# Two rows of the batch to a partition in a six-layer cross network

## The reference

```python
def step(x, wb):
    wi, bi = wb
    xw = jnp.matmul(x, wi)
    x_new = x0 * xw + bi + x
    return (x_new, None)
x, _ = jax.lax.scan(step, inputs, (w, b))
```

## Time and profile before

| | |
|---|---|
| median of 3 runs | 1281.35 us (1281.14 to 1282.9) |
| profiled execution | 1280.2 us |
| its span, first to last instruction | 1278.4 us |
| mean granted TensorE clock | 0.782 of full |
| VectorE busy | 1150.2 us, 90% |
| TensorE busy | 780.7 us, 61% |
| ScalarE busy | 102.7 us, 8% |
| moved by DMA | 537.28 MB, 420 GB/s on the mean |

### The profile page before, as it was taken

How to read it: one execution, slowest core, us unless ns; L and a number is a source line. 1 busy time by engine, 2 the same in 40 slices (tenths; PEclk the granted TensorE clock), 3 DMA queues, 4 the chain that set the end, 5 groups by cost and what they waited for, 6 DMA issues and landing times.

```text
span 1278.4 us, 20057 instructions
## 1 busy us (share of the span) xinstructions
PE 780.7 (61%) x9114; PEld 728.6 (57%) x9114; DVE 1150.2 (90%) x526; ACT 102.7 (8%) x345; POOL 4.3 (0%) x17
## 2 busy tenths in 40 slices
PE   8666666555656655556555665665655665665653
PEld 4666566555556655555545565565655654665653
DVE  5999999898988988989889898898998988989896
ACT  3000000000000000000000000000000000000010
POOL 1000000000000000000000000000000000000000
PEclk9877787887877778778787777777777778678677
DMA  9999999999999999999999999999999999999996
GB/s 385 416 380 428 430 431 431 429 427 429 433 429 431 431 430 432 430 431 424 421 424 425 418 427 421 424 425 422 427 424 421 424 423 425 425 423 425 426 421 286
DMA packets 37385, 537.28 MB, mean 420 GB/s; under 512 B 4168, under 2 KB 4168, under 8 KB 4728
## 3 DMA queue, kind: packets, MB, share of 16 engines
q1 hardware_dynamic: 18432, 268.44, 50.1%
q10 hardware_dynamic: 18936, 268.64, 49.3%
HBM read 268.63 MB, written 268.44 MB: 420 GB/s over the span
## 4 chain that ended last, share of the span: by engine, by line
DMA 72%; DVE 15%; PE 8%; issue 3%; ACT 1%; DVEq 0%
DMA out_dram<-tiles 56%; DMA tiles<-in_r_inputs_dram 15%; DVE tiles L286 8%; DVE blocks L264 7%; PE dots L401 6%; ACT spread L197 1%; PE dots L359 1%; PE scratch L339 1%; DMA tiles<-in_L_rec_w_dram 0%; PE strips L334 0%; PE strips L349 0%; ACT c_last L189 0%; PE turned L370 0%; DVE scale L275 0%; DVEq L42 0%
## 5 line engine op out<-in xcount | busy, mean ns | idle before, releaser
L401 PE MATMUL dots<-blocks,weights 128*64 128x128 f32 x7808 | 662.6, 349 | 380.8 <-DVE blocks L264 380.6
L401 PEld LDWEIGHTS dots<-blocks,weights 128*64 128x64 f32 x7808 | 628.7, 185 | 405.3 <-DVE blocks L264 405.2
L264 DVE STREAM_TRANSPOSE blocks<-tiles 128x2048 f32<-128x2048 f32 x256 | 576.0, 2288 | 100.1 <-issue 100.1
L286 DVE SCALAR_TENSOR_TENSOR tiles<-tiles,scale,c_last 128x4096 f32<-128x4096 f32 (+1 forms) x131 | 571.9, 4368 | 0.2
L197 ACT ACTIVATE spread<-dots,group_mask 128x128 f32<-128x128 f32 (+1 forms) x268 | 75.2, 363 | 1062.6 <-PE dots L401 1020.3
L370 PE MATMUL turned<-layer_sel,spread 128*128 128x8 f32 x512 | 68.1, 258 | 85.5 <-ACT spread L197 85.5
L370 PEld LDWEIGHTS turned<-layer_sel,spread 128*128 128x128 f32 x512 | 62.3, 191 | 101.4 <-issue 95.6
L359 PE MATMUL dots<-blocks,weights 128*64 128x64 f32 x768 | 32.4, 266 | 11.0 <-DVE blocks L264 11.0
L359 PEld LDWEIGHTS dots<-blocks,weights 128*64 128x64 f32 x768 | 31.7, 180 | 12.9 <-issue 12.9
L205 ACT ACTIVATE growth<-turned,ones 128x16 f32<-128x16 f32 (+1 forms) x67 | 18.3, 273 | 85.0 <-PE turned L370 85.0
L275 DVE TENSOR_TENSOR_SCAN scale<-growth,cw 128x6 f32<-128x6 f32 x128 | 13.3, 142 | 8.9 <-ACT growth L205 8.9
(11 more groups left out here) (25 smaller groups left out, 11.3 us busy)
## 6 DMA issues: line engine op xcount, KB each, us to landing
tiles<-in_r_inputs_dram SPq DMA_DIRECT2D x128, 2048.0 KB, 14.9
out_dram<-tiles ACTq DMA_DIRECT2D x127, 2048.0 KB, 25.5
out_dram<-tiles ACTq DMA_DIRECT2D x4, 512.0 KB, 7.0
tiles<-in_L_rec_w_dram ACTq DMA_DIRECT2D x1, 96.0 KB
tiles<-in_L_rec_b_dram ACTq DMA_DIRECT2D x1, 96.0 KB
```

The source lines that it names most:

```text
L264: nc.vector.transpose(blocks[:, p % PLACES, :], source).then_inc(blocks_ready, 1)
L286: nc.vector.scalar_tensor_tensor(out=tiles[:, s, at], in0=tiles[:, s, at], scalar=scale[:, u % 2, t, L - 1:L], in1=c_last[:, at], op0=ALU. ...
L401: last = nc.tensor.matmul(dots[at:at + KM * Q, :, :, :], weights[:, c * CH // Q + k:c * CH // Q + k + KM, :], place[:, :, k * Q:(k + KM) * Q],
```

## The change

The rows are laid out in pairs: partition p of a pair of tiles holds rows 2p and 2p + 1 of a stretch of 256 rows, which lie side by side in HBM. There are five slots, each for a pair of tiles (4 MB), so 20 MB in place of 16. A pair is loaded by one DMA of 4 MB, 32 KB to a partition; singles are still loaded one tile at a time. A store is still one tile, now every second row of 16 KB. A slot's next load waits for both of its stores.

Room for this comes from three places. `blocks` has two places in place of four. `c_last` is gone: its lower half is in SBUF (`c_low`), its upper half stays in PSUM (`c_high`, the same memory as `scratch`), and `finish` works in two halves, one with each. `quarter_sum` is gone: the biases are also loaded as rows (`b_rows`, four small DMAs), and TensorE sums six rows with `ones`.

VectorE's order changes. A pair now has all four transposes together, then the finish of tile 1 of the unit before, then the scan and the finish of tile 0 of the same pair. ScalarE spreads, makes the growth, then stores tile 1 of the unit before and tile 0 of this one.

```diff
-PLACES = 4
+PLACES = 2
+PIECES_OF_PAIR = 4
-N_SLOTS = 8
+N_SLOTS = 5
...
+    x_pairs = x.rearrange("(q p t) d -> q p t d", p=P, t=TB)
+    out_pairs = out.rearrange("(q p t) d -> q p t d", p=P, t=TB)
...
+            for q in range(n_all_pairs):
+                s = q % N_SLOTS
...
+                if q >= N_SLOTS:
+                    for t in range(TB):
+                        sp.wait_ge(y_stored[s][t], 16 * stores(q - N_SLOTS))
+                if in_singles(q):
+                    for t in range(TB):
+                        sp.dma_start(tiles[:, s, t, :], x_pairs[q, :, t, :]).then_inc(x_landed[s][t], 16)
+                else:
+                    sp.dma_start(tiles[:, s, :, :], x_pairs[q]).then_inc(x_landed[s][0], 16)
...
             act.dma_start(strips_w, w_strips).then_inc(w_landed, 16)
-            act.dma_start(strips_b, b_strips).then_inc(b_landed, 16)
...
             for j in range(G):
-                nc.scalar.activation(quarter_sum[:, j, :], ones[:], ACT.Copy,
-                                     scale=of_quarter[:, j:j + 1]).then_inc(quarter_sum_ready, 1)
+                act.dma_start(b_rows[j * Q:j * Q + L, :, :], b_halves[j]).then_inc(b_landed[j], 16)
+            act.dma_start(strips_b, b_strips).then_inc(strips_b_landed, 16)
...
+            act.wait_ge(bias_summed, 1)
+            nc.scalar.copy(c_low[:], c_high).then_inc(c_low_ready, 1)
...
-            keep_bias(0)
-            spread_dots(0)
-            keep_bias(1)
             act.wait_ge(cw_all_ready, 1)
             nc.scalar.copy(cw[:], strips[:, 0, 0:LP]).then_inc(cw_ready, 1)
+            spread_dots(0)
             make_growth(0)
             for u in range(1, n_units):
...
+                spread_dots(u)
+                make_growth(u)
+                store(tiles_of(u)[0] - 1)
+                if tiles_of(u)[1] == TB:
+                    store(tiles_of(u)[0])
...
-                parts = 1 if n < n_tiles - 1 else PIECES
+                parts = 2 if n < n_tiles - 1 else STORE_PARTS
...
+                    c = c_low[:, at] if i < parts // 2 else c_high[:, i * width - HALF:(i + 1) * width - HALF]
...
                 wait_tiles(u)
-                transpose_pieces(u, range(2))
+                transpose_pieces(u, range(2 * n_of))
                 if u == 1:
-                    dve.wait_ge(scratch_copied, 2)
+                    dve.wait_ge(c_low_ready, 1)
+                    dve.wait_ge(bias_summed, 2)
                     dve.wait_ge(cw_ready, 1)
-                scan(u - 1)
-                finish(u - 1, 0)
+                if n_before == 1:
+                    scan(u - 1)
+                finish(u - 1, n_before - 1)
                 if n_of == TB:
-                    transpose_pieces(u, range(2, 2 * TB))
-                for t in range(1, n_before):
-                    finish(u - 1, t)
+                    scan(u)
+                    finish(u, 0)
...
-                    last = nc.tensor.matmul(scratch[:, j, :], quarter_sum[0:STRIPS, j, :],
-                                            strips_b[:, h * BANK:(h + 1) * BANK], start=True, stop=True)
+                    last = nc.tensor.matmul(scratch[:, j, :], ones[j * Q:j * Q + L, :], b_rows[j * Q:j * Q + L, h, :],
+                                            start=True, stop=True, tile_position=(j * Q, 0))
...
-                for c in range(PLACES):
-                    pe.wait_ge(blocks_ready, n * PLACES + c + 1)
-                    place = blocks[:, c, :].rearrange("p (t n) -> p t n", t=TB)
+                for c in range(PIECES_OF_PAIR):
+                    pe.wait_ge(blocks_ready, n * PIECES_OF_PAIR + c + 1)
+                    place = blocks[:, c % PLACES, :].rearrange("p (t n) -> p t n", t=TB)
```

More of the change, by code:

```diff
@@ L120, in tiles_of, with in_singles, loads, stores @@
             return u + n_pairs * (TB - 1), 1
+        def in_singles(q):
+            return q * TB < HEAD or q * TB >= n_tiles - TAIL
         def pieces_before(u):
             return 2 * tiles_of(u)[0]
+        def loads(q, t):
+            return sum(1 for k in range(q % N_SLOTS, q + 1, N_SLOTS) if t == 0 or in_singles(k))
+        def stores(q):
+            return q // N_SLOTS + 1
         def weights_of(g):
@@ new lines, in _ @@
+                make_growth(u)
+                store(tiles_of(u)[0] - 1)
+                if tiles_of(u)[1] == TB:
+                    store(tiles_of(u)[0])
+            last_slot = (n_all_pairs - 1) % N_SLOTS
+            for i in range(STORE_PARTS):
+                at = slice(i * D // STORE_PARTS, (i + 1) * D // STORE_PARTS)
+                act.wait_ge(tiles_done, n_tiles + i)
+                act.dma_start(out_pairs[n_all_pairs - 1, :, TB - 1, at],
+                              tiles[:, last_slot, TB - 1, at]).then_inc(y_stored[last_slot][TB - 1], 16)
@@ L241, in _ @@
+            for q in range(n_all_pairs - N_SLOTS, n_all_pairs):
+                s = q % N_SLOTS
+                for t in range(TB):
+                    parts = STORE_PARTS if q * TB + t == n_tiles - 1 else 1
+                    act.wait_ge(y_stored[s][t], 16 * (stores(q) - 1 + parts))
         @block.vector
@@ L261, in transpose_pieces @@
                         dve.wait_ge(blocks_used, p - PLACES + 1)
-                    source = tiles[:, s, c * PIECE:(c + 1) * PIECE] if n_of == 1 else \
-                        tiles[:, s:s + TB, c * CH:(c + 1) * CH]
+                    source = tiles[:, s, first % TB, c * PIECE:(c + 1) * PIECE] if n_of == 1 else \
+                        tiles[:, s, :, c * CH:(c + 1) * CH]
                     nc.vector.transpose(blocks[:, p % PLACES, :], source).then_inc(blocks_ready, 1)
             def wait_tiles(u):
-                first, n_of = tiles_of(u)
-                for n in range(first, first + n_of):
-                    dve.wait_ge(x_landed[n % N_SLOTS], (n // N_SLOTS + 1) * 16)
+                first = tiles_of(u)[0]
+                q, t = first // TB, first % TB
+                dve.wait_ge(x_landed[q % N_SLOTS][t], 16 * loads(q, t))
             def scan(u):
-                first, n_of = tiles_of(u)
+                n_of = tiles_of(u)[1]
                 dve.wait_ge(growth_ready, u + 1)
@@ L279, in finish @@
                 n = tiles_of(u)[0] + t
-                s = n % N_SLOTS
+                tile = tiles[:, n // TB % N_SLOTS, n % TB, :]
                 dve.wait_ge(scale_ready, n + 1)
-                parts = 1 if n < n_tiles - 1 else PIECES
+                parts = 2 if n < n_tiles - 1 else STORE_PARTS
                 width = D // parts
@@ L285, in finish @@
                     at = slice(i * width, (i + 1) * width)
-                    nc.vector.scalar_tensor_tensor(out=tiles[:, s, at], in0=tiles[:, s, at],
-                                                   scalar=scale[:, u % 2, t, L - 1:L], in1=c_last[:, at],
-                                                   op0=ALU.mult, op1=ALU.add).then_inc(tiles_done, 1)
+                    c = c_low[:, at] if i < parts // 2 else c_high[:, i * width - HALF:(i + 1) * width - HALF]
+                    done = nc.vector.scalar_tensor_tensor(out=tile[:, at], in0=tile[:, at],
+                                                          scalar=scale[:, u % 2, t, L - 1:L], in1=c,
+                                                          op0=ALU.mult, op1=ALU.add)
+                    if parts == STORE_PARTS or i == parts - 1:
+                        done.then_inc(tiles_done, 1)
             dve.wait_ge(w_copied, W_BANKS)
@@ L404, in _ @@
                                                 start=(c == 0 and k < parts * KM),
[L405 removed]
+                                                stop=(c == PIECES_OF_PAIR - 1 and k >= CH // Q - parts * KM),
                                                 tile_position=(0, at))
```

76 lines of the change are left out of this document (34 added, 42 removed).

## The result

The changed kernel takes 1335.46 us (median of 4 runs, 1333.8 to 1335.95), the kernel before 1281.49 us: a ratio of 1.0417, 95% interval 1.0399 to 1.0435. Forecast were 1334 us and a range of 1300 to 1354. They also show a second cost, in the transfers, that the prediction held at zero.

The account below looks back on a forecast made before the run. Bytes bound the kernel before; after, VectorE's chain would: first pair at 35.4 us, 61 periods of 20.5 us, then singles, last parts and last store to a span of 1332, plus 2.95: 1334 us, range 1300 to 1354.

Parts of the forecast that it names:

- Bound and slack before: Kernel before is bound by bytes, 19.8 us per pair late in the run; VectorE has some 1.7 us per pair to spare.
- Chain through two places and the same pair's scan: A pair's loop becomes one chain through VectorE, TensorE, ScalarE and back, D + 11.9 us long, and takes over as bound.
- D: Time from the start of a pair's transpose 0 to the end of TensorE's piece 1, taken as 8.6 us.
- The rest of the chain: After D: transpose 3, TensorE's piece 3, spread, turn, growth, scans and the finish of tile 0; D + 11.95 in all.
- Cut of a finish: Splitting each finish of 4096 columns into two of 2048 costs 0.14 us, 4.59 in place of 4.45 us.
- the rival on PSUM reads: Half-finishes reading the bias from PSUM are slower by d per tile; at d = 0.3, 27 us more, 1361 us; 6%.
- The period: Time from one pair to the next, 20.5 us for 61 pairs, above the DMA's 19.8 us.
- Head and tail: First pair starts at 35.4 us, 61 periods end at 1285.9, singles and last parts at 1328.5, last store takes 3.5 us.
- Transfers at zero: Larger loads and row-skipping stores: gain or loss of up to 18 us, counted as zero because VectorE's chain bounds.
- bytes stay the bound: Rival: D below 7.6 us on the mean, period under 19.5 us, 1262 to 1281 us, say 1277; chance 6%.
- DMA share 0.96: Sign in the profile after: DMA queues fall to about 0.96 full in mid-run, as the chain bounds.
- Five slots: A slot is held 91 us against 102.5 us available, so loads stay ahead; rival of too few slots, 1395 us, 4%.

Follow-up runs that it names:

- runs 7 to 10: Changed kernel, old order, with: untied 2 MB loads, 1278.8 us; tied 2 MB loads, 1282.34; 4 MB loads in 16 KB packets, 1278.5; 32 KB packets both ways, 1282.49.
- run 2: Kernel before with the changed kernel's order and two places, its own slots, transfers and one-part finishes kept: 1331.97 us, ratio 1.039.
- 3 and 4: Kernel before with the new order but four places: 1283.18 us; kernel before with two places only, order kept: 1281.42 us.
- run 5: Changed kernel with seven extra matmuls into an unused PSUM bank behind each pair's turn, keeping TensorE busy: 1316.44 us, ratio 1.026.
- run 6: Changed kernel with each finish in four parts in place of two: 1336.3 us.
- run 1: Changed kernel with VectorE's and ScalarE's order of before, its layout, slots, transfers and two places kept: 1364.17 us, ratio 1.0623.
- the copy: Changed kernel's transfers alone, all arithmetic left out: 1309.87 us, against 1252.35 us for the transfers of the kernel before alone.
- run 9: Changed kernel with the old order and one 4 MB load per pair in 16 KB packets (rows p and p + 128): 1278.5 us, ratio 0.9976.
- run 10: Changed kernel with the old order and pairs also stored whole, 32 KB packets both ways: 1282.49 us, ratio 1.0016.

## Why the prediction was right

- **Bound and slack before.** Right: with the chain cut and like packets, runs 7 to 10 are back within 0.25% of before.
- **Chain through two places and the same pair's scan.** Shown by run 2 (3.9% by itself), and by 3 and 4, which take away one link each and lose nothing.
- **Its terms.** D was taken as 8.6; the fourth transpose starts 8.70 us in, so D is 8.6. The rest of the chain is 20.48 - 8.70 = 11.78 us, forecast 11.85 from the same point. Cut of a finish: 0.14 forecast; measured from the first half's start to the next transpose it is 669.49 - 664.96 = 4.53 us, against 698.77 - 694.37 = 4.40 before (rows below), 0.13. Wait for growth 0.24 us, forecast some 0.2. The PSUM half costs 2325 against 2315 ns, d = 0.01: the rival on PSUM reads falls, and the 0.065 us that the prediction worked out from the Trainium skill ("VectorE: DVE Perf Modes", the TRN2 errata) is not seen here, where one of the two tensors read lies in PSUM.

```profile
694.37 4.49 DVE L286 SCALAR_TENSOR_TENSOR tiles<-tiles,scale,c_last 128x4096 f32<-128x4096 f32 x1
698.77 2.31 DVE L264 STREAM_TRANSPOSE blocks<-tiles 128x2048 f32<-128x2048 f32 x1
```

- **The period.** 20.5 forecast, 20.48 measured. The low level of the clock in piece 0 was argued from the longer idle (7.5 us forecast, 7.43 measured), and run 5 shows that it makes most of the chain's waits. That the sum hit to 0.02 us is partly luck. D = 8.6 was picked from the upper half of a spread, not worked out, and run 6 shows that the period does not follow the sum: with some 0.25 us more or 0.12 us less in the rest of the chain it is the same 20.48. Adding terms to a fixed D was the wrong form, though no error came of it here; with the finish in four it forecast 1360 us, 24 us too many.
- **Head and tail.** First pair at 34.65 us (35.4 forecast), last pair's end at 1283.89 (1285.9), end 1333.5 (1332): the last store took 6.6 us, not 3.5. These misses nearly cancel. The prediction's last sum is also 1 us short: 1332 + 2.95 is 1335, not 1334.
- **Transfers at zero.** The step that was wrong: "As DVE's chain is the bound and leaves the queues 4% of slack, the value that counts is zero at both ends", with 18 us as the most that could be lost. In run 1 the loss is 83 us, in the copy 58 us. The total was right because the two costs overlap and, at 20.48 us a pair, nothing waited for a load, so the chain hid this one; that was not foreseen. Why the same transfers keep up with that period under the new order, and in run 1 need 21.7 us a pair (8.39 MB at 387 GB/s), is open. The rival "bytes stay the bound", priced at 1277, was mis-sized for the same reason: run 5 comes nearest to its condition, with D at 6.5 where the clock is high, and took 1316 us. The fixed part of each DMA that the prediction took from the Trainium skill ("DMA: Bandwidth & Descriptors", anatomy of one DMA) is fitted there on DMAs that GpSimd issues; here SyncE and ScalarE issue them. Nothing hangs on it: 4 MB per load with like packets (run 9) gained 0.2%.
- **DMA share 0.96.** Wrong: 1.00 in mid-run, and 50.7% + 47.3% = 98.0% over the span. In the slower kernel the same bytes took more packet time, so the share stayed full. Run 2 shows it with packets of 16 KB: 0.510 x 16 x 1331.6 = 10,870 us of engine time for the loads, 10,250 in before. Why a packet takes longer there is not shown.
- **Five slots.** A pair's load takes 17.2 us and a store 13.3 us to landing after, within what was allowed (25.5 us and twice 14.9 us), and no wait for loads is left.

## What to carry to other kernels

Halving a ring of buffers is free or costs 4% by the order of the work around it: look at what the producer does between writing place i and place i + 2, and whether the consumer is idle long enough before to start at its low clock. When loads and stores share the DMA engines, keep the packets of both directions alike: a copy with loads of 32 KB and stores of 16 KB took 58 us more than one of 1252 us with 16 KB both ways, and in the full kernel of run 1 the unlike sizes cost some 82 us against run 10, while 16 KB both ways and 32 KB both ways (with the engines' work) stayed with the kernel before. A DMA share of 1.00 alone does not say that bytes bind: ask whether anyone waits for a load, and whether the GB/s are those that full queues reach elsewhere.

## What was not expected of the hardware

Two changes that each cost some 4 to 6% gave 4.2% together, and undoing the one that was understood made the kernel slower by 29 us. The period of a chain that holds a change of TensorE's clock stayed at 20.48 us in three kernels whose other terms differ by up to 0.4 us. In the copies, loads and stores of unlike packet sizes moved 416 GB/s with the DMA share at 1.00, and like ones 431; the unlike ones then ended with 30 us at a share of 0.13.
